# The causal mask of an attention kernel, moved from products on TensorE to additions on VectorE

## The reference

```
scores = jnp.einsum('bqhd,bkhd->bhqk', qq, kk) * scale
causal = jnp.tril(jnp.ones((S, S), dtype=bool))
scores = jnp.where(causal[None, None], scores, jnp.finfo(scores.dtype).min)
probs = jax.nn.softmax(scores, axis=-1)
y = jnp.einsum('bhqk,bkhd->bqhd', probs, v).reshape(B, S, H)
```

## Time and profile before

| | |
|---|---|
| Median of 3 runs | 4385.75 us (4384.99 to 4388.7) |
| Profiled execution, span (first to last instruction) | 4383.6 us |
| Mean granted TensorE clock | 0.934 of full speed |
| TensorE matmul, weight load | 86%, 64% of the span |
| VectorE | 67% of the span |
| ScalarE | 57% of the span |
| GpSimd | 50% of the span |

### The profile page before, as it was taken

How to read it: one execution, slowest core, us unless ns; L and a number is a source line. 1 busy time by engine, 2 the same in 40 slices (tenths; PEclk the granted TensorE clock), 3 DMA queues, 4 the chain that set the end, 5 groups by cost and what they waited for, 6 DMA issues and landing times.

```text
span 4383.6 us, 70750 instructions
## 1 busy us (share of the span) xinstructions
PE 3756.6 (86%) x22264; PEld 2785.4 (64%) x22264; DVE 2958.8 (67%) x5456; ACT 2514.4 (57%) x6505; POOL 2196.1 (50%) x1115
## 2 busy tenths in 40 slices
PE   5888888888888883999869888998999999989987
PEld 2344444444444442777758787887887887887876
DVE  3444454545444532222269999999999999999998
ACT  1433343434433441333368887887887887887874
POOL 3223333333333322000048877877778778778775
PEclk7889999999998996999989999999999999999998
DMA  3322222322232213666622222222222222222221
GB/s 99 91 76 84 80 84 87 94 80 79 93 97 81 88 41 99 201 210 209 198 88 76 97 84 76 93 88 76 93 88 76 93 88 76 93 86 78 93 78 42
DMA packets 286603, 419.96 MB, mean 96 GB/s; under 512 B 78262, under 2 KB 250679, under 8 KB 263673
## 3 DMA queue, kind: packets, MB, share of 16 engines
q1 hardware_dynamic: 273048, 381.12, 26.5%
q0 software_dynamic: 12288, 33.57, 2.2%
q10 hardware_dynamic: 864, 0.10, 0.0%
HBM read 330.63 MB, written 83.17 MB: 94 GB/s over the span
## 4 chain that ended last, share of the span: by engine, by line
DVE 33%; issue 11%; PE 2%; ACT 2%; DVEq 1%; POOL 1%; DMA 0%; SPq 0%; POOLq 0%; ACTq 0%
DVE m_S L1756 7%; DVE m_PR L1756 7%; DVE m_S L1748 7%; DVE m_PR L1748 7%; ACT m_dA L1645 1%; DVE m_ub L1733 1%; DVE m_yz L1767 1%; PE m_F L1866 1%; DVE m_x L1717 1%; DVE m_th_x L1725 1%; DVEq L1747 1%; PE m_Y L1904 1%; POOL m_ub L1536 0%; PE m_F L1864 0%; PE m_F L1840 0%
## 5 line engine op out<-in xcount | busy, mean ns | idle before, releaser
L1536 POOL TENSOR_TENSOR m_ub<-m_Bb,m_dtx 128x2048 f32<-128x2048 f32 x254 | 1156.3, 4564 | 321.4 <-PE m_Y L1904 219.6
L1645 ACT ACTIVATE m_dA<-m_dt,m_a_neg 128x128 f32<-128x128 f32 x4096 | 1211.1, 388 | 132.2 <-DVE m_S L1756 131.8
L1904 PE MATMUL m_Y<-m_ub,m_ident 128*128 128x128 f32 x8192 | 972.3, 281 | 90.6 <-DVE m_ub L1733 90.4
L1904 PEld LDWEIGHTS m_Y<-m_ub,m_ident 128*128 128x128 f32 x8192 | 955.5, 197 | 102.0 <-DVE m_ub L1733 102.0
L543 ACT ACTIVATE f_pt<-f_X 128x512 f32<-128x512 f32 (+1 forms) x704 | 371.3, 555 | 735.1 <-PE f_X L845 696.6
L618 DVE TENSOR_REDUCE f_nm<-f_Y 128x1 f32<-128x512 f32 (+3 forms) x896 | 434.4, 531 | 366.9 <-PE f_Y L845 342.6
L1748 DVE SCALAR_TENSOR_TENSOR m_PR<-m_dA,m_S 128x512 f32<-128x512 f32 x512 | 355.8, 695 | 54.4 <-issue 29.9
L1748 DVE SCALAR_TENSOR_TENSOR m_S<-m_dA,m_PR 128x512 f32<-128x512 f32 x512 | 354.8, 693 | 12.0
L1756 DVE CUSTOM_DVE_ANT_1 m_PR<-m_PR,m_ub 128x512 f32<-128x512 f32 x512 | 353.4, 690 | 9.9 <-issue 9.8
L1756 DVE CUSTOM_DVE_ANT_1 m_S<-m_S,m_ub 128x512 f32<-128x512 f32 x512 | 353.3, 690 | 0.0
L828 PE MATMUL f_Y<-f_kst,f_qst 96*128 96x512 bf16 (+3 forms) x1024 | 258.4, 333 | 109.2 <-DVE f_nm L618 90.9
(11 more groups left out here) (234 smaller groups left out, 6365.7 us busy)
## 6 DMA issues: line engine op xcount, KB each, us to landing
m_Bb<-m_bc_dram SPq DMA_DIRECT2D x64, 1024.0 KB, 4.5
m_Cb<-m_bc_dram SPq DMA_DIRECT2D x64, 1024.0 KB, 6.2
f_parts_dram<-f_parts SPq DMA_DIRECT2D x32, 768.0 KB, 4.0
f_kst<-f_parts_dram SPq DMA_DIRECT2D x192, 128.0 KB, 2.6
f_qst<-f_parts_dram SPq DMA_DIRECT2D x192, 128.0 KB, 2.6
e_rows<-sorted_rows SPq DMA_DIRECT2D x70, 256.0 KB, 2.7
e_wg<-Wg SPq DMA_DIRECT2D x70, 256.0 KB, 2.9
e_wu<-Wu SPq DMA_DIRECT2D x70, 256.0 KB, 3.9
```

Of the source, the lines that this page charges most:

```text
L1536: pool.tensor_tensor(ub[:, h, i, :, :], Bb[:, s, :, :], dtx[:, m, None, s * SN:(s + 1) * SN].to_broadcast([P, NST, SN]), ALU.mult).then_in ...
L1645: last = act.activation(dA[:, h, i, n, :], dtt[:, par, m, s * SN:(s + 1) * SN], ACT.Exp, scale=a_neg[:, m, n:n + 1])
L1904: last = pe.matmul(Y[:, i * SN:(i + 1) * SN], ident[:, :], ub[:, h, 1 + i, n, :], start=False, stop=(n == NST - 1), skip_group_check=True)
```

## The change

The mask products are gone. `row_max` is now one `tensor_tensor_reduce` for each row piece: it adds a mask tile to the columns in place, in PSUM, and takes the minimum of the negated sum, which is the negated maximum. The mask tile `causal` has 512 columns, zeros and the triangle in the last 128, and its last n columns are used for a piece of n. What was one reduce for a pair of heads is two instructions. For the transposed scores VectorE has a new share of each `s2` item: it adds the triangle `later` in place to all diagonal blocks of the bank, and a new semaphore `hidden` tells ScalarE that the exp may start. TensorE raises the bank's full semaphore with the last score product. Two smaller edits make room and order: `th` (tanh) and `sg` (gate) share one buffer, and the wait of VectorE for the down projection of the round before moves to ScalarE. `ORDER` is the same as before.

```diff
-    mask_q = sb("f_mask_q", [P, P], bf16)
-    mask_k = sb("f_mask_k", [P, P], bf16)
+    causal = sb("f_causal", [P, SEQ], bf16)
+    later = sb("f_later", [P, P], bf16)
...
-    th = sb("f_th", [P, NS, SEQ])
     sg = sb("f_sg", [P, NS, SEQ])
+    th = sg
...
                 act.wait_ge(pv_done, NG * TT * b + max(i - 1, 0))
+                act.wait_ge(hidden, len(S2_AT) * b + S2_AT[i, j] + 1)
                 read(("s2", i, j), probs(i, j), lambda bank: bank[:, 0:probs_width(i)], ACT.Exp)
...
-            def row_max(k, out, cols, last=True):
-                ins = dve.tensor_reduce(out, cols(full(k, r)), AX.X, ALU.max, negate=True)
+            def row_max(k, out, c0, n, last=True):
+                if c0 == 0:
+                    dve.wait_ge(*filled(k, r))
+                    dve.sem_inc(taken)
+                cols = bank_of(k, r)[:, c0:c0 + n]
+                ins = dve.tensor_tensor_reduce(out=cols, in0=cols, in1=causal[:, SEQ - n:SEQ], scale=-1.0, scalar=-MASKED,
+                                               op0=ALU.add, op1=ALU.min, accum_out=out)
...
-                    row_max(("s1", i, j, 0), nm[:, 1, h:h + 2], lambda bank: bank[:, :].rearrange("p (h n) -> p h n", h=2))
+                    row_max(("s1", i, j, 0), nm[:, 1, h:h + 1], 0, 256, last=False)
+                    row_max(("s1", i, j, 0), nm[:, 1, h + 1:h + 2], 256, 256)
+            if kind == "s2":
+                kb = i % TT
+                heads, n = HG // N_S2[kb], SEQ - P * kb
...
+                cols = full(("s2", i, j), r)[:, 0:heads * n].rearrange("p (h n) -> p h n", h=heads)[:, :, 0:P]
+                dve.tensor_tensor(cols, cols, later[:, None, :].to_broadcast([P, heads, P]), ALU.add).then_inc(hidden, 1)
...
-                    full(("s1", i, j, 0), r, hide(bank, 384, P, 1, mask_q))
+                    full(("s1", i, j, 0), r, scores(bank, 0, h + j, 3, p))
...
-                full(("s2", i, j), r, hide(bank, 0, SEQ - P * kb, heads, mask_k))
+                full(("s2", i, j), r, last)
```

More of the change, by code:

```diff
@@ L143, in build_attn @@
                     S2_ITEMS.append(("oc", g - 1, 0))
+    S2_AT = {(q, n): at for at, (q, n) in enumerate((q, n) for q in range(NG * TT) for n in range(N_S2[q % TT]))}
     STAGE = {kind: 2 for kind in ("xload", "bn", "h1", "h1a", "T", "lat", "kq", "split", "mid", "keep", "stack")}
@@ L246, in build_attn @@
     nm_stacked = sem("f_nm_stacked")
+    hidden = sem("f_hidden")
     pv_done = sem("f_pv_done")
@@ L440, in masks_and_ones @@
                                      base=0, pattern=[[-1, P]], channel_multiplier=1))
[L441 to L442 removed]
+            fixed(pool.memset(causal[:, :], 0.0))
+            fixed(pool.affine_select(out=causal[:, SEQ - P:SEQ], in_=causal[:, SEQ - P:SEQ], compare_op=ALU.is_ge, fill=MASKED,
                                      base=0, pattern=[[-1, P]], channel_multiplier=1))
[L444 to L445 removed]
+            fixed(pool.memset(later[:, :], 0.0))
+            fixed(pool.affine_select(out=later[:, :], in_=later[:, :], compare_op=ALU.is_ge, fill=MASKED,
                                      base=0, pattern=[[1, P]], channel_multiplier=-1))
@@ L605, in do @@
                 if not isinstance(b, int) or b > 0:
-                    act.wait_ge(*used(("g", i), before_(r)))
+                    act.wait_ge(*filled(("d", 1), before_(r)))
                 act.activation(th[:, i, :], bank_of(("g", i), r)[:, :], ACT.Tanh, scale=0.5).then_inc(th_ready, 1)
@@ L827, in scores @@
             n = P * (qb + 1)
-            pe.matmul(bank[:, c0:c0 + n], qst[p][0:KS, h, qb * P:(qb + 1) * P], kst[p][0:KS, h, 0:n],
-                      start=(c0 == 0), stop=False, skip_group_check=True)
+            return pe.matmul(bank[:, c0:c0 + n], qst[p][0:KS, h, qb * P:(qb + 1) * P], kst[p][0:KS, h, 0:n],
+                             start=(c0 == 0), stop=True, skip_group_check=True)
         def scores_t(bank, c0, h, kb, p):
             n = SEQ - P * kb
[L834 to L845, removed]
+            return pe.matmul(bank[:, c0:c0 + n], kst[p][:, h, kb * P:(kb + 1) * P], qst[p][:, h, kb * P:SEQ],
+                             start=(c0 == 0), stop=True, skip_group_check=True)
         def values(q, b, r):
@@ L870, in attend @@
                     bank = free(("s1", i, j, 0), r)
-                    scores(bank, 0, h + j, 3, p)
-                    full(("s1", i, j, 0), r, hide(bank, 384, P, 1, mask_q))
+                    full(("s1", i, j, 0), r, scores(bank, 0, h + j, 3, p))
                     bank = free(("s1", i, j, 1), r)
                     scores(bank, 0, h + j, 2, p)
-                    scores(bank, 384, h + j, 0, p)
-                    full(("s1", i, j, 1), r, hide(bank, 256, P, 2, mask_q))
+                    full(("s1", i, j, 1), r, scores(bank, 384, h + j, 0, p))
                 else:
@@ L879, in attend @@
                     scores(bank, 0, h, 1, p)
-                    scores(bank, 256, h + 1, 1, p)
-                    full(("s1", i, j, 0), r, hide(bank, P, 2 * P, 2, mask_q))
+                    full(("s1", i, j, 0), r, scores(bank, 256, h + 1, 1, p))
             if kind == "nmt":
@@ L899, in attend @@
                 for n in range(heads):
-                    scores_t(bank, n * (SEQ - P * kb), g * HG + j * heads + n, kb, p)
-                full(("s2", i, j), r, hide(bank, 0, SEQ - P * kb, heads, mask_k))
+                    last = scores_t(bank, n * (SEQ - P * kb), g * HG + j * heads + n, kb, p)
+                full(("s2", i, j), r, last)
             if kind == "pv":
```

13 lines of the change are left out of this document (7 added, 6 removed).

## The result

The changed kernel takes 4586.35 us (median of 4 runs, 4573.72 to 4593.81); the kernel before, run beside it, 4385.37 us. The ratio is 1.0471 (95% interval 1.045 to 1.0491): slower by 201 us, where 144 had been predicted and 4425 to 4650 us given as the range. The profiled execution of the changed kernel took 4573.72 us, its span is 4571.9 us, 188.3 more than before, and its mean granted TensorE clock 0.88 instead of 0.934.

A forecast was written before the change was run, and what follows sets the result against it. TensorE was taken to carry each attention round, with VectorE half idle. Steps of +7.4 us and +2 for the clock made +9.4 a full round, 132 us in 14 rounds plus 12 at the ends: 4530 us, range 4425 to 4650.

The forecast's parts named there:

- (b): Transposes of h1 to those of h2: TensorE's saving mostly given back by fills waiting behind dearer maxima, -0.1 us a round.
- (c): From transposes of h2 to the router rank chain's end: maxima and adds delay the gate product and chain, +1.8 us.
- (d): Behind the rank chain: TensorE's X fill waits for an exp whose add stands behind the chain, +2.5 us a round.
- (e): From behind the rank chain up to the prefix products: TensorE is dense again and saves, -1.0 us a round.
- hidden adds, faster: Rival: all adds and maxima fall into VectorE's idle time, TensorE gains 7 us in 15 rounds, 4281 us; chance 0.06.
- (f): Prefix chain: the X fill waits for an exp whose add stands behind VectorE's five prefix instructions, +2.9 us a round.
- (g): Split of the maxima to the round's end: an add more behind it, but much wait already used up, -0.6 us.
- (a): Round start to transposes of h1: exp waits for maxima and an add, dearer triple and add ahead, +1.9 us.
- clock term: Two new gaps ahead of dense products bring TensorE's lower clock level: +2 us a round, ends 0 and +8.
- the walk: One round followed step by step with the trace's times, later or earlier than before: sum +7.4 us, clock not included.
- rival "clock": New gaps keep TensorE at its lower level through dense products: +6 to +10 us more a round, 4608 to 4664; chance 0.17.
- the forecast's 4480 to 4600: Whole kernel: the prediction's main case, a time of 4480 to 4600 us around the likeliest 4530; chance 0.54.

The follow-up runs named there:

- e1: The kernel before without the mask products and nothing in their place (causal mask within diagonal blocks left out): 4421.14 us, ratio 1.0105.
- e4: The changed kernel with the 84 products a round put back on TensorE, of a tile of zeros: 4561.77 us, ratio 1.0411.
- e5: The changed kernel with the router's rank chain cut in four pieces and VectorE's prefix instructions five positions later: 4501.13 us, ratio 1.0294.
- e9: The kernel before with 24 idle products a round (identity times ones) put ahead of TensorE's known waits: 4356.15 us, ratio 0.9964.

## Why the prediction was right in direction and short in size

**(b) held**: +0.1 against -0.1. TensorE's saving is not seen anywhere: in e1, where nothing stands against it, the four stretches sum to 103.4 us, 2.6 more than before.

**(c), mis-sized.** In the pair of rounds that the rows show, the gate product started 8.42 us after T2 before (857.46 to 865.88) and the chain ended 8.25 later (873.92 + 0.21). After, TensorE's timeline:

```profile
840.38 1.96 PE L794 MATMUL f_Z<-f_ident,f_h 128*128 128x128 f32 x8 [0.92 <-ACT f_h L569]
843.84 3.42 PE L929 MATMUL f_Z<-f_w_r,f_h2T 128*128 128x7 f32 x16
848.13 3.62 PE L945 MATMUL f_Z<-f_h2T,f_wg 128*128 128x512 f32 x4
...
863.39 0.61 PE L850 MATMUL f_X<-f_qst,f_kst 99*128 99x256 bf16 x2 [1.68 <-ACT f_pt L546]
863.79 3.41 PE L945 MATMUL f_Z<-f_h2T,f_wu 128*128 128x512 f32 x4
...
881.20 0.61 PE L850 MATMUL f_X<-f_qst,f_kst 99*128 99x512 bf16 x1 [2.92 <-ACT f_pt L546]
```

and VectorE's (gate product, end of the chain, the add behind it; then the add behind the prefix instructions):

```profile
852.52 0.69 DVE L766 SCALAR_TENSOR_TENSOR f_sg<-f_sg,f_Z 128x512 f32<-128x512 f32 x1 [3.28 <-ACT f_sg L611]
...
862.39 0.21 DVE L745 TENSOR_REDUCE f_info<-f_picked 128x8 f32<-128x56 f32 x1
862.52 0.29 DVE L675 TENSOR_TENSOR f_X<-f_X,f_later 128x128 f32<-128x128 f32 x1
...
880.11 0.33 DVE L675 TENSOR_TENSOR f_X<-f_X,f_later 128x128 f32<-128x128 f32 x1
```

T2 to the gate product is 12.14 us, +3.7 where +0.8 stood: the first three groups of TensorE's rows run at the lower level and take 4.1 us longer than before (9.00 against 4.94), as in e1. The gate product to the chain's end is 10.08 us, +1.8 where +1.0 stood. So (c) was +5.5 in this pair, not +1.8. The round before is one of its quick ones: in five of the eleven this first part takes 10.0 to 13.3 us, not 8.4. Over the eleven rounds the first part is +2.1 (9.8 to 11.8 us) and the second +1.0 (8.45 to 9.45), +3.1 together. The excess of the first part is the clock: e1, without any add, takes 11.4 us there at the same granted clock as after (0.57 in both, 0.83 before), and e4, with the products back, 10.6 at 0.81, which is the +0.8 of the forecast.

**(d) and (e): mechanism right, size too small.** The X fill starts at 863.39, 0.79 us after the chain's end at 862.60, with the add at 862.52 ahead of ScalarE's exp and a wait of 1.68 us for it. That was the point on which "hidden adds, faster" hung, and it fell out against it. From the chain's end to the prefix products it takes 14.28 us, 10.83 before: +3.5 where +1.5 stood (over the eleven rounds 13.8, +3.0; e1 10.6). The up projection right behind the fill takes 3.41 us at the lower level, 1.88 in e5 at the upper: 1.5 of the missing 2. The lower level follows the wait here, as the prediction had it, and the products do not prevent it: e4 takes 14.5 us, with an up projection of 3.28 us behind a wait of 2.33 in one of its rounds.

**(f) held almost to the number.** The X fill comes 4.32 us after the prefix products (876.88 to 881.20), forecast 4.5, 1.58 before: +2.7 where +2.9 stood. **(g)** does not show: from this fill to the transposes of the split maxima 4.7 us, 4.9 before.

**(a), too small.** From the split to T1, which is (a) and the end of the old round, +4.7 us where +1.9 stood. From the first X fill of a round to T1, in one round each at whose start the loop doesn't turn, 16.2 us became 19.9 (1006.02 to 1022.18, and 897.88 to 917.77): +3.7, at a granted clock of 0.71 from split to T1. The clock is little of it: e1 has 0.72 in this stretch and is 0.5 us longer than before, and e4, back at 0.80, is not shorter than the changed kernel. What is left by these runs is VectorE's queue; none divides it further. Where the loop of two rounds turns there is a little more. The earlier trace rows showed VectorE idle for 4.52 us "issue" at that place, and I read over it, because VectorE had nothing to do then. After, on VectorE, ScalarE and TensorE:

```profile
1012.45 0.17 DVE L680 COPY f_mvx<-f_sc 128x4 f32<-128x4 f32 x1 [5.70 <-issue]
...
1016.99 0.50 DVE L675 TENSOR_TENSOR f_X<-f_X,f_later 128x128 f32<-128x128 f32 x2 [4.29 <-issue]
...
1017.40 1.08 ACT L546 ACTIVATE f_pt<-f_X 128x512 f32<-128x512 f32 x2 [6.99 <-DVE f_X L675]
...
1018.06 0.61 PE L850 MATMUL f_X<-f_qst,f_kst 99*128 99x512 bf16 x1 [3.56 <-ACT f_pt L546]
```

VectorE first has to work off the last adds of the old round and then idles twice, and now two banks of X hang on it. From the split to T1, the rounds with the turn take 32.4 us before and 37.4 after (means of five), those without it 27.3 and 31.7 (means of six): the turn itself became dearer by 0.7 us, some 0.3 a round. No run isolates this.

**The clock term is the step that failed, and (a) was mis-sized beside it.** The clock was put at +2 a round (ends 0 and +8), caused by the two new gaps (d) and (f). e1 has neither gap, and its clock falls to 0.82 all the same; its round is 2.6 us longer than before, where the walk alone, with nothing in VectorE's queue, gives only savings. The cause that I did not see is the removal itself: with the products in the stream, TensorE ran at its upper level more often (e1 against before; e4 and e9 the other way round). By the round, +13.4, the measured value lies between the forecast (+9.4) and the rival "clock" (+15.4 to +19.4). Of the 6 us above the walk's +7.4, 1.3 stand in the clock part of (c), 1.5 in (d) and (e), where part of it is the clock behind the wait, and 2.8 in (a), mainly the queue.

That the time came out inside the forecast's 4480 to 4600 is in part luck, as errors stood against each other. The new maxima cost VectorE 2.9 us a round and not 8.7, and a cast in the split became 1.9 us shorter (below), which no term had counted; what either is worth in the kernel's time no run shows. In busy time, VectorE's extra 14.4 us a round are the adds alone (32 x 0.306 + 8 x 0.441 + 4 x 0.717 = 16.2) less that cast. The rounds at either end were put about right: 14 rounds of 13.35 are 187 us and the phase is 203 longer, so that they cost some 16 us, where 12 stood. But what follows the phase is 14 us shorter in the profiled execution, and no term had that.

## What to carry to other kernels

Work that is taken from the busiest engine is worth its start-to-start time at most, and on TensorE it can be worth less than nothing, since its granted clock follows: leave the work out alone, as in e1, before finding another engine for it. Average only over rounds that hold the same items, and look at more than one pair: single rounds of the kernel before differ by 6 us from T2 to the prefix products. An operation put between two engines that hand banks to each other costs its place in the third engine's queue far more than its own time: list what stands ahead of it there, long dependent chains and the loop's turn included. Where TensorE's clock falls during known waits, products that go nowhere but fill these waits can pay: 0.36% here, more than any form of the change.

## What was not expected of the hardware

- Removing 84 small products a round (0.26 to 0.27 us of busy time each) lowered the granted clock from 0.92 to 0.82 and made the kernel 1.05% slower (e1); 24 products into waits raised it to 0.96 and made it 0.36% faster (e9).
- The read of the accumulator behind an add-and-minimum takes 142 ns and starts together with the next instruction: three maxima take 1.38 us, start to start (899.52 to 900.90), against 1.26 for three plain reduces (868.35 to 869.61).
- A cast of 64 columns on VectorE takes 2066 ns before, in all 8 rounds, where it starts next to a GpSimd instruction of 2.1 us (888.27 and 888.16), and 185 ns after, where GpSimd is idle. VectorE's rows by form, before and then after, 400 to 1200 us:

```profile
L669 DVE CAST f_nm_part<-f_nm 128x64 bf16<-128x64 f32 x8 | 16.5, 2066 | 0.0
```

```profile
L688 DVE CAST f_nm_part<-f_nm 128x64 bf16<-128x64 f32 x7 | 1.3, 185 | 0.0
```
